# Moving the products of probabilities and values into pairs on TensorE: quarters 0 and 1 behind the seventh score group, 2 and 3 in the next step

## The reference, cut to what matters

```python
qp = (q @ w_q + b_q).reshape(B, Nq, H, D).transpose(0, 2, 1, 3)      # B=16, Nq=112, H=16, D=16
kvp = (kv @ w_kv + b_kv).reshape(B, Nkv, 2, H, D).transpose(2, 0, 3, 1, 4)   # Nkv=375
kp, vp = kvp[0], kvp[1]
attn = softmax(einsum('bhqd,bhkd->bhqk', qp, kp) * SCALE)
out = einsum('bhqk,bhkd->bhqd', attn, vp).transpose(0, 2, 1, 3).reshape(B, Nq, C)
x = x + out @ w_out + b_out
x = x + ffn(layernorm(x))       # mean gate over a batch position, then two mixed layers 256 -> 1024 -> 256
```

## Time and profile before

| what | value |
|---|---|
| median of 3 runs | 951.06 us (950.96 to 954.01) |
| the profiled execution: its time | 955.64 us |
| the profiled execution: span of the core | 953.6 us |
| PE busy, share of the span | 901.2 us, 95% |
| DVE, ACT, POOL busy | 467.8, 244.7, 236.1 us |
| mean granted TensorE clock | 0.987 of full speed |
| scores(0, 0) starts, scores(15, 0) starts | 59.3 us, 286.5 us into the span |

### The profile page before, as it was taken

How to read it: one execution, slowest core, us unless ns; L and a number is a source line. 1 busy time by engine, 2 the same in 40 slices (tenths; PEclk the granted TensorE clock), 3 DMA queues, 4 the chain that set the end, 5 groups by cost and what they waited for, 6 DMA issues and landing times.

```text
span 953.6 us, 17240 instructions
## 1 busy us (share of the span) xinstructions
PE 901.2 (95%) x6250; PEld 747.1 (78%) x6250; DVE 467.8 (49%) x799; ACT 244.7 (26%) x453; POOL 236.1 (25%) x365
## 2 busy tenths in 40 slices
PE   2888999999987899999999999999999999999998
PEld 2766888888865688888888888878888888888887
DVE  6676778777774465555555555543331112111121
ACT  2646777777755200000000001012211001000000
POOL 6443555555513214111111111312203003000000
PEclk9899999999998999999999999999999999999999
DMA  7469776767740370010001000201002001000000
GB/s 188 99 160 237 191 171 179 171 182 182 195 104 9 99 265 23 22 44 22 22 22 44 22 22 22 88 23 43 24 23 89 0 1 45 0 0 3 25 22 28
DMA packets 43799, 74.10 MB, mean 78 GB/s; under 512 B 12379, under 2 KB 33963, under 8 KB 43763
## 3 DMA queue, kind: packets, MB, share of 16 engines
q1 hardware_dynamic: 43762, 73.61, 28.0%
HBM read 56.41 MB, written 17.01 MB: 77 GB/s over the span
## 4 chain that ended last, share of the span: by engine, by line
PE 84%; DMA 5%; DVE 3%; ACT 2%; issue 2%; POOL 2%; SPq 2%; ACTq 0%; POOLq 0%; DVEq 0%
PE banks L308 40%; PE banks L1513 32%; PE banks L1250 3%; PE banks L1232 3%; PE banks L1209 3%; DMA k_stack<-k_dram 3%; DMA w_f<-in_wv 1%; PE banks L1495 1%; DMA k_dram<-k_parts 1%; ACT probs L696 1%; DVE x_norm L1002 1%; DVE maxima L971 1%; POOL k_parts L575 1%; PE banks L1261 1%; SPq L378 0%
## 5 line engine op out<-in xcount | busy, mean ns | idle before, releaser
L308 PE MATMUL banks<-w_parts,xt_parts 128*128 128x512 f32 x1344 | 305.8, 390 | 0.0
L308 PEld LDWEIGHTS banks<-w_parts,xt_parts 128*128 128x128 f32 x1344 | 252.1, 188 | 53.6 <-issue 1.1
L1513 PE MATMUL banks<-w_parts,h_high 128*128 (+1 forms) x896 | 240.9, 391 | 1.6 <-DVE h_low L1129 1.6
L1098 DVE SCALAR_TENSOR_TENSOR acc<-banks,gates,acc 128x512 f32<-128x512 f32 x196 | 147.1, 751 | 119.4 <-PE banks L308 119.4
L1513 PEld LDWEIGHTS banks<-w_parts,h_high 128*128 128x128 f32 x896 | 167.4, 188 | 35.7 <-DVE h_low L1129 1.8
L594 POOL TENSOR_TENSOR w_parts<-w_raw,w_parts 128x1024 fp32r<-128x1024 f32 (+1 forms) x32 | 76.4, 2394 | 416.2 <-ACT w_parts L733 416.2
L1123 DVE SCALAR_TENSOR_TENSOR y<-banks,gates,y 128x256 f32<-128x256 f32 x112 | 54.2, 484 | 235.7 <-PE banks L1513 231.4
L1513 PE MATMUL banks<-w_parts,h_low 128*128 (+1 forms) x448 | 138.2, 390 | 0.0
L971 DVE TENSOR_REDUCE maxima<-banks 112x2 f32<-112x750 f32 x128 | 117.6, 934 | 27.0 <-PE banks L1209 24.2
L733 ACT ACTIVATE w_parts<-w_raw 128x1024 fp32r<-128x1024 f32 (+1 forms) x32 | 33.6, 1058 | 354.6 <-PE banks L308 261.0
L696 ACT ACTIVATE probs<-banks 128x448 f32<-128x448 f32 x192 | 100.2, 544 | 23.0 <-PE banks L1232 20.9
(11 more groups left out here) (112 smaller groups left out, 738.0 us busy)
## 6 DMA issues: line engine op xcount, KB each, us to landing
w_raw<-in_w SPq DMA_DIRECT2D x32, 512.0 KB, 3.3
k_dram<-k_parts SPq DMA_DIRECT2D x16, 576.0 KB, 3.1
k_stack<-k_dram SPq DMA_DIRECT2D x32, 288.0 KB, 3.8
k_stack<-k_dram SPq DMA_DIRECT2D x32, 192.0 KB, 4.1
c_raw<-in_ctx_t SPq DMA_DIRECT2D x16, 375.0 KB, 3.8
k_stack<-k_dram SPq DMA_DIRECT2D x32, 96.0 KB, 4.4
b_rows<-gate_dram SPq DMA_DIRECT2D x12, 256.0 KB, 4.5
q_dram<-q_parts SPq DMA_DIRECT2D x16, 168.0 KB, 4.3
```

The lines of the kernel that those rows point to most:

```text
L308: last = pe.matmul(out_ap, left(a, k), right(b, k), start=(n == 0), stop=(n == 3 * tiles - 1))
L1098: dve.scalar_tensor_tensor(out=acc[:, t, 512 * s:512 * s + 512], in0=banks[:, t % NB1, :], scalar=gate_col, in1=base[:, 512 * s:512 * s + ...
L1513: last = pe.matmul(banks[:, t % 2, :], h_part[a][:, t, 2 * c + k, :], w, start=(n == 0), stop=(n == 3 * OT - 1))
```

## The change

In each step, `weigh_values(s, 0)` moves from behind `scores(s, 5)` to behind `scores(s, 6)`, directly in front of `weigh_values(s, 1)`, which stays. `weigh_values(s, 2)` leaves the place between `scores(s, 9)` and `scores(s, 10)` and is done in the next step, directly in front of `weigh_values(s, 3)`, which already stood there. In step 0 (`second_step`) only quarter 2 moves; step 16 gets it for batch 15. Only PE's list changes; all semaphores count as before.

```diff
@@ second_step
                 max_scores(nxt, 4)
-                weigh_values(b, 2)
                 scores(b, 10)
@@ last_steps
                     last = Batch(B - 1)
+                    weigh_values(last, 2)
                     weigh_values(last, 3)
@@ step
                 scores(s, 0)
+                weigh_values(last, 2)
                 weigh_values(last, 3)
                 max_transpose(s, 1)
...
                 scores(s, 5)
-                weigh_values(s, 0)
                 max_scores(nxt, 4)
                 output_back(last)
                 scores(s, 6)
+                weigh_values(s, 0)
                 weigh_values(s, 1)
                 max_transpose(nxt, 0)
...
                 scores(s, 9)
-                weigh_values(s, 2)
                 scores(s, 10)
                 max_scores(nxt, 7)
                 scores(s, 11)
```

## The result

The changed kernel took 963.0 us (961.64 to 963.67, 4 runs) against 951.93 us before (950.96 to 954.01, 4 runs): ratio 1.0098, 95% interval 1.0072 to 1.0125. So the change makes the kernel about 1% slower, and the interval is clear of 1. The forecast was 961.7 us, a ratio of 1.0112 to the 951.06 us it started from. The profiled execution took 962.48 us with a span of 960.4 us.

The account below looks back on a forecast made before the run. PE, busy 95% of the span, was taken as the bound. A steady step gained 0.97 us (-0.42 work, +0.77 and +0.61 waits); with the other steps +10.6, so 951.1 + 10.6 = 961.7 us, range 956 to 968.

Parts of the forecast that it names:

- PE's saving: Each step, two lone product blocks fewer (-1.62 us) and two joined ones more (+1.20): PE's own work shrinks 0.42 us.
- First wait: At max_scores(nxt, 4), PE idles 0.77 us a step for DVE's reduce_max(nxt, 2), which hangs on the token transposes.
- Second wait: At scores(s, 11), PE idles 0.61 us a step for exp(s, 9), which ACT does behind key_copy.
- Steady step: Steps 5 to 12: each grows 0.97 us, from 14.61 to 15.58, together 7.8 us.
- The other steps: Steps 1 to 4 and 13 to 15: shift 1.44 us after step 4, 9.2 after 12, 10.3 after 13, 10.6 finally.
- Lone price: Rival: joined blocks cost as much as lone ones, 0.81 us; 13 steps add 5.5, giving 967.2 us; chance 0.12.
- Gain: Rival: no new waits at max_scores(nxt, 4) and scores(s, 11); 0.42 us a step saved, 945.6 us; chance 0.06.
- Only one wait: Rival: ACT gives exp(s, 9) in time, so only the max_scores(nxt, 4) wait comes; +3.3, 954.4 us; chance 0.10.
- The clock: Rival: PE's new idle brings half clock, 3.2 us in each of 12 steps; 19 us more, some 981; chance 0.07.

Follow-up runs that it names:

- pair01_only: Kernel before with only product blocks 0 and 1 paired, weigh_values(s, 0) moved behind scores(s, 6); 959.1 us, ratio 1.0043.
- dve_first: Changed kernel with reduce_max(nxt, 2) on DVE moved in front of the low part of the tokens; 957.77 us, ratio 1.0028 to before.
- pair23_only: Changed kernel with weigh_values(s, 0) back behind scores(s, 5), so only quarters 2 and 3 are paired; 956.45 us, ratio 1.0020 to before.
- act_first: Changed kernel with exp(s, 9) moved in front of key_copy(new, 0) on ACT; 963.43 us, ratio 1.0108 to before.
- fill_second: Changed kernel with exp(s, 9) before key_copy(new, 0) on ACT and scores(s, 9) before key_project(new, 0) on PE; 961.74 us, ratio 1.0109 to before.
- after_again: The changed kernel as it is, measured and profiled a second time; 965.06 us, ratio 1.0124 to before.
- exp3_lone: lone_filled with exp(s, 3) also moved in front of tokens_high(old) on ACT; 951.81 us, ratio 0.9989 to before; run again 951.03 us, 0.9961.
- lone_filled: Kernel before, four product blocks left alone, with the DVE, ACT and key_project reorderings of dve_first and fill_second; 953.7 us, ratio 0.9996.
- pe_fill01: Kernel before, PE only: quarters 0 and 1 paired behind scores(s, 6), max_scores(nxt, 4) moved behind the pair; 954.85 us, ratio 1.0012.
- fill_both: Changed kernel with the edits of dve_first and fill_second together; 955.98 us, ratio 1.0035 to before.
- exp3_pair: fill_both with exp(s, 3) also moved in front of tokens_high(old) on ACT; 958.1 us, ratio 1.0036 to before.

## Why the prediction was right

**PE's saving.** 0.42 us a step forecast. The joined block costs 0.58 (1.18 less 0.60), so it is 1.62 less 1.16: 0.46. Busy time over steps 5 to 12 fell by only 1.14 us, 0.14 a step (115.68 to 114.54), because 0.16 us of each of the two new waits is booked as busy: 0.46 less 0.32. The starts are the measure. The Trainium skill (TensorEngine Tiling, Key Properties) says that changing the tiling mode drains TensorE; the trace agrees with it in that two lone blocks cost 1.62 us and two joined ones 1.16, but no run here tells a drain from another cost of the change, such as that from bf16 to fp32. The saving is real on PE; it didn't decide the time.

**First wait.** Forecast 0.77 us at max_scores(nxt, 4), put down to DVE maxima. Measured 0.77; pair01_only shows it alone, dve_first takes it down to 0.10 by moving its releaser. Shown.

**Second wait.** Forecast 0.61 at scores(s, 11). Measured 0.61; pair23_only shows it alone, act_first moves it to key_project(new, 1), fill_second removes 0.39 of a steady step. Shown.

**Steady step.** Forecast 15.58 (from 14.61), measured 15.53 and 15.64 in turn (from 14.61 and 14.71): +0.92 instead of +0.97, the difference being the 0.58 for 0.60 once in each half and what follows from it. Steps 5 to 12: +7.2 us instead of 7.8.

**The other steps.** Here the terms were mis-sized. Compared profile to profile, the changed kernel starts scores(0, 0) 1.5 us sooner (57.78 against 59.30), which has nothing to do with the change. Steps 1 to 4 were to add 1.4 us. In the profiles, scores(0, 0) to scores(5, 0) took 79.61 us before and 82.23 after: +2.6, with 2.0 in step 1, where the half clock came that I had not counted. Step 13 was to add 1.1 us and gave 2.5 back. I had argued that its load of keys goes with scores(12, 11) and so its wait stays; the longest transfer of that load landed 6.0 us after its issue instead of 6.9, for a reason not tested. Steps 14 and 15, up to the token transpose of step 16, were to add 0.3 and added 0.9 (it starts at 309.82 instead of 303.17, a shift of 6.65 where that of scores(14, 0) is 5.8). Profile to profile the change is 962.48 less 955.64, +6.8 us, against +11.1 between the medians: the profiled execution of before was 3.7 us over the median of 951.93 (4.6 over the 951.06 that I started from), that of after 0.5 under its own. I carried those 4.6 over as if they lay outside the change. The 16.1 us of step 13 are probably a part of them, and then a wait and a half clock that I counted as fixed were those of one execution. So the mechanism and the 7.2 us of the steady steps are shown, and that the total of +10.6 comes so near to +11.1 is partly luck: errors of both signs in the other steps are small beside the 7.2.

**The rivals.** Lone price: refuted, 0.58 for a joined block. Gain: refuted, the waits come to 1.38 where 0.42 would have been the turning point. Only one wait: refuted. The clock: it stayed at 1.00 through the steady steps with 0.77, 0.61 and 0.37 us of idle in each. In step 1 it was at 0.51 from 84.9 to 88.3 us, behind a wait of 1.98. The length of such a wait alone doesn't tell: behind 1.95 us in after_again (83.25), 1.95 in fill_second (267.57) and 2.15 in dve_first (87.44) the granted clock stayed at 1.00.

## What to carry to other kernels

In a pipeline whose order is written out by hand, a block on the busiest engine is also the cover for someone else's operation. Before moving it, find the next wait behind its old place and the slack there. With the 0.06 us from a release to a start taken off, that is 0.03 and 0.20 us here (the prediction's 0.09 leaves the 0.06 in). If the block (0.81 us) is larger than the slack, the engine waits for the difference, and the move loses when these waits (1.38 us) are more than what it saves (0.46). The small gain lay elsewhere, in order changes that leave the products where they were: exp3_lone moves exp(s, 3) and exp(s, 9) on ACT, one reduction on DVE and key_project on PE. All but exp(s, 3) together brought nothing (lone_filled), so the gain comes with the wait in front of scores(s, 5), the one that the profile had shown from the start. Whether moving exp(s, 3) alone would do wasn't run.

## What the runs showed of the hardware

At full clock, a block of 24 MATMUL records with 32 stationary columns (fp32) between operations with 112 or 128 (bf16) costs TensorE 0.09 us on entering (0.30 less 0.21) and 0.12 on leaving (0.72 less 0.60; for a pair 1.30 in pe_fill01 less 1.18). A second block joined to the first costs 0.58.

VectorE's x_norm (112x256 fp32, SBUF to SBUF) takes 0.41 us in the steady steps of before and 1.69 us in step 7 of fill_both, where it starts just behind a GpSimd operation that reads and writes SBUF:

```profile
169.82 1.62 POOL L571 TENSOR_TENSOR k_rest<-k_f,k_parts 128x752 f32<-128x752 f32 x1
```

It ends at 171.44, x_norm at 171.59. In step 6 of the same kernel x_norm is first, by 0.10 us:

```profile
155.41 0.41 DVE L1002 TENSOR_SCALAR x_norm<-x_mid,mean_var,rstd 112x256 f32<-112x256 f32 x1 [1.29 <-POOL rstd L566]
...
155.51 1.80 POOL L571 TENSOR_TENSOR k_rest<-k_f,k_parts 128x752 f32<-128x752 f32 x1
```

Then x_norm keeps its 0.41 us, and the GpSimd operation takes 1.80 instead of 1.62. The Trainium skill (SBUF — State Buffer, SBUF: two separate sides) says that whichever of the two engines starts first gets the port pair that they share for its whole instruction, if the VectorE operation runs in a mode that uses both of its ports or has two inputs in SBUF. The trace agrees in that the later of the two is the longer one in both steps; the mode of x_norm isn't in the profile. It ends only 0.15 us behind the GpSimd operation, less than its 0.41, so either a part of it runs before or the recorded ends, which are rough for GpSimd, are off. A shift of 0.1 to 0.2 us in where such an operation starts can thus cost 1.3 us on VectorE, and this goes with the longer steps of fill_both and exp3_pair.
